# Row maxima of an attention kernel as fp16 parts, split on GpSimd and transposed once

## What is computed

```python
x = x + 0.5 * ffn(layernorm(x))
x = x + attention(layernorm(x))
x = x + 0.5 * ffn(layernorm(x))

# attention: 16 query heads, 4 key/value groups, head size 16, causal
scores = jnp.einsum('bhqd,bhkd->bhqk', q, k) * (1.0 / np.sqrt(d))
scores = jnp.where(causal[None, None, :, :], -jnp.inf, scores)
attn = jax.nn.softmax(scores, axis=-1)
out = jnp.einsum('bhqk,bhkd->bhqd', attn, v)

# feed-forward: weights quantised to three values
hidden = jax.nn.silu(up) * gate
```

## Time and profile before

| | |
|---|---|
| Median of 3 runs | 603.82 us (603.62 to 603.99) |
| Profiled execution | 604.03 us, its span 602.3 us |
| TensorE busy | 566.0 us, 94% of the span |
| VectorE, ScalarE busy | 485.8 us (81%), 412.1 us (68%) |
| GpSimd busy | 176.7 us (29%) |
| Chain that ended last, by engine | PE 79%, DVE 10%, ACT 6% |

### The profile page before, as it was taken

How to read it: one execution, slowest core, us unless ns; L and a number is a source line. 1 busy time by engine, 2 the same in 40 slices (tenths; PEclk the granted TensorE clock), 3 DMA queues, 4 the chain that set the end, 5 groups by cost and what they waited for, 6 DMA issues and landing times.

```text
span 602.3 us, 12457 instructions
## 1 busy us (share of the span) xinstructions
PE 566.0 (94%) x4276; PEld 344.9 (57%) x4276; DVE 485.8 (81%) x1865; ACT 412.1 (68%) x775; POOL 176.7 (29%) x229
## 2 busy tenths in 40 slices
PE   2869999999999989999999999998999999999998
PEld 2336556655666755656566656554445666656666
DVE  6998988889875889888988897888597687756654
ACT  4637756765655378898888888887767656765742
POOL 3015201101530035555545455667501101101100
PEclk9999999999999999999999999999999999999999
DMA  8701001100205151414141424231201111211112
GB/s 313 219 19 35 19 19 36 35 19 19 36 17 125 37 111 56 92 54 93 56 90 58 95 62 92 77 59 30 45 1 36 53 54 36 70 54 53 36 35 71
DMA packets 71679, 37.90 MB, mean 63 GB/s; under 512 B 33984, under 2 KB 71104, under 8 KB 71616
## 3 DMA queue, kind: packets, MB, share of 16 engines
q1 hardware_dynamic: 71616, 37.11, 24.3%
HBM read 18.22 MB, written 10.49 MB: 48 GB/s over the span
## 4 chain that ended last, share of the span: by engine, by line
PE 79%; DVE 10%; ACT 6%; issue 2%; POOL 2%; DMA 1%; DVEq 0%; POOLq 0%; ACTq 0%
PE bank L1112 33%; PE bank L1124 17%; PE bank L1211 7%; PE bank L1279 5%; PE bank L1270 5%; PE bank L1238 5%; ACT shared L566 3%; PE bank L1293 2%; PE bank L1284 2%; DVE sm_out L951 2%; PE bank L1103 1%; DVE hid L814 1%; DVE hl L829 1%; PE bank L1249 1%; POOL xn L395 1%
## 5 line engine op out<-in xcount | busy, mean ns | idle before, releaser
L951 DVE CUSTOM_DVE_ANT_0 sm_out<-bank,mask 128x256 f16<-128x256 f32 (+1 forms) x512 | 153.6, 352 | 25.7 <-PE bank L1238 23.4
L456 ACT ACTIVATE silu<-bank,w_scale 128x512 f32<-128x512 f32 x128 | 87.3, 683 | 117.0 <-PE bank L1112 116.1
L814 DVE SCALAR_TENSOR_TENSOR hid<-silu,h_unit,bank 128x512 f32<-128x512 f32 x128 | 95.0, 742 | 62.5 <-ACT silu L456 62.1
L566 ACT ACTIVATE shared<-bank,qk_scale 128x512 f32<-128x512 f32 x192 | 121.5, 681 | 21.7 <-PE bank L1270 20.8
L1124 PE MATMUL bank<-wT_down,hh 128*128 128x256 f16 x512 | 118.2, 273 | 1.8 <-DVE hl L829 1.6
L1124 PE MATMUL bank<-wT_down,hl 128*128 128x256 f16 x512 | 118.2, 273 | 0.0
L1112 PE MATMUL bank<-xh,wT_gate 128*128 128x512 f16 x256 | 97.1, 379 | 4.4 <-DVE hid L814 4.4
L1112 PE MATMUL bank<-xh,wT_up 128*128 128x512 f16 x256 | 98.0, 383 | 1.2 <-DVE xl L758 1.2
L829 DVE TENSOR_TENSOR hl<-hid,hh 128x512 f16<-128x512 f32 x128 | 98.1, 767 | 0.0
L1112 PE MATMUL bank<-xl,wT_up 128*128 128x512 f16 x256 | 98.0, 383 | 0.0
L404 POOL TENSOR_TENSOR xnl<-xn,xnh 128x1024 f16<-128x1024 f32 x13 | 27.7, 2134 | 238.1 <-ACT xn L493 180.4
(11 more groups left out here) (115 smaller groups left out, 750.3 us busy)
## 6 DMA issues: line engine op xcount, KB each, us to landing
q_st<-q_scratch SPq DMA_DIRECT2D x32, 256.0 KB
q_scratch<-q_hl SPq DMA_DIRECT2D x16, 256.0 KB, 2.2
out_dram<-x SPq DMA_DIRECT2D x7, 512.0 KB, 2.9
x<-in_x_dram SPq DMA_DIRECT2D x1, 3072.0 KB, 15.6
k_scratch<-k_hl SPq DMA_DIRECT2D x16, 128.0 KB, 2.4
k_st<-k_scratch SPq DMA_DIRECT2D x16, 128.0 KB
x<-in_x_dram SPq DMA_DIRECT2D x2, 512.0 KB, 4.6
shared<-in_w_up_t_dram SPq DMA_DIRECT2D x2, 512.0 KB, 6.2
```

What stands on the lines that cost most here:

```text
L456: act.activation(silu[:, e % 2, :], U[e % 2][:, :], ACT.Silu, scale=w_scale[:, 0:1]).then_inc(silu_ready, 1)
L566: act.activation(prob[:, place % 2, i, :], score_bank(n, i)[:, :], ACT.Exp, scale=qk_scale[:, 4:5]).then_inc(exp_done, 1)
L814: dve.scalar_tensor_tensor(out=hid[:, e % 4, :], in0=silu[:, e % 2, :], scalar=h_unit[:, 0:1], in1=GT[e % 2][:, :], op0=ALU.mult, op1=ALU. ...
L951: ins = dve.tensor_tensor_reduce(sm_out[:, i, cols], SM[i][:, cols], mask[:, S - size:S], 1.0, MASKED, ALU.add, ALU.max, rowmax[:, seq_par ...
```

## The change

The split of the maxima moves ahead of the transposes. VectorE now takes the minimum of the negated and scaled scores, so that `rowmax` holds minus the maximum in the units of the product. At the head of groups 0 and 2, ahead of the masks, GpSimd makes both fp16 parts from it in the layout of the queries (`max_parts`: a conversion and a subtraction of 128x16, with a wait of its own between them). TensorE transposes both parts and both query tiles at once (fp16, 128x32) in groups 1 and 3, ScalarE copies the 32x128 result once, ahead of the copy of the outputs (VectorE does so in the one place where it copies the outputs), and SyncE loads rows of 128 instead of 256 elements, in groups 1 and 3. `q_st` has an axis of its own for the sequence, and the scratch read of the second sequence is issued in group 1 of the next even sequence.

```diff
-        q_st = sb("q_st", [P, 2, H, TC], F16)
+        q_st = sb("q_st", [P, 2, 2, H, S], F16)
...
-                sp.wait_ge(mxlo_ready, 2 * b + half + 1)
+                sp.wait_ge(mx_ready, 2 * b + half + 1)
...
-                    sp.dma_start(q_st[64 + part:65 + part, par, heads, cols],
-                                 mx_hl[:, half, part, :]).then_inc(mx_loaded[half], 16)
+                    sp.dma_start(q_st[64 + part:65 + part, par, seq, heads, :].rearrange("o h (t q) -> o (h t) q", t=QT),
+                                 mx_hl[part * QT * HH:(part + 1) * QT * HH, half, :]).then_inc(mx_loaded[half], 16)
...
-                        if g in (0, 2) and not (last and k == 3):
-                            if last and k == 2 and g == 2:
+                        if g in (1, 3) and not (last and k == 3):
+                            if last and k == 2 and g == 3:
                                 x_parts(NC, 0)
                             load_max(b + 1, k + 1, g // 2)
...
-                            sp.wait_ge(st_ready, 3 * G * (b + 1))
-                            read_scratch(c + 2, par, 1)
+                        if not odd and g == 1 and (k or pair) and not (last and k):
+                            sp.wait_ge(st_ready, 3 * G * b)
+                            read_scratch(c + 1, 1 - par, 1)
...
+            step(pool.tensor_copy(ident16[:, :], ident32[:, :]))
...
-            def max_rest(b, half):
-
-                pool.wait_ge(mx_ready, 2 * b + half + 1)
-                if not isinstance(b, int) or b > 0:
-                    pool.wait_ge(mx_loaded[half], 32 * b)
-                pool.tensor_tensor(mx_hl[:, half, 1, :], mx_32[:, half, :], mx_hl[:, half, 0, :],
+            def max_parts(b, half):
+
+                pool.wait_ge(sm_done, 3 * (G * b + 2 * half + 2))
+                if b:
+                    pool.wait_ge(mxT_ready, 2 * b + half - 1)
+                heads = rowmax[:, b % 2, :, half * HH:(half + 1) * HH].rearrange("p t h -> p h t")
+                pool.tensor_copy(mx_q[:, half, 0, :, :], heads).then_inc(mxhi_ready, 1)
+                pool.wait_ge(mxhi_ready, 2 * b + half + 1)
+                pool.tensor_tensor(mx_q[:, half, 1, :, :], heads, mx_q[:, half, 0, :, :],
                                    ALU.subtract).then_inc(mxlo_ready, 1)
...
+                        if g in (0, 2) and not end:
+                            max_parts(b + 1, g // 2)
                         if odd and g in (2, 3):
                             add_output(b - 1, g - 2, 3 - g)
                         if not (end and g == 3):
                             causal(4 * b + g + 1, (g + 1) % 2)
-                        if g in (0, 2) and not end:
-                            max_rest(b + 1, g // 2)
...
-                act.activation(mx_hl[:, half, 0, :], maxima[0:HH, :], ACT.Copy, scale=-1.0 / MAX_UNIT)
-                act.activation(mx_32[:, half, :], maxima[0:HH, :], ACT.Copy,
-                               scale=-1.0 / MAX_UNIT).then_inc(mx_ready, 1)
+                act.activation(mx_hl[:, half, :], maxima, ACT.Copy).then_inc(mx_ready, 1)
...
-                        if g in (0, 2) and not end:
+                        if g in (1, 3) and not copied_by_vector(n):
                             max_copy(b + 1, g // 2)
...
-                    ins = dve.tensor_tensor_reduce(sm_out[:, i, cols], SM[i][:, cols], mask[:, S - size:S], 1.0, MASKED,
-                                                   ALU.add, ALU.max, rowmax[:, seq_par, qt, h:h + 1])
+                    ins = dve.tensor_tensor_reduce(sm_out[:, i, cols], SM[i][:, cols], mask[:, S - size:S], -1.0 / MAX_UNIT,
+                                                   -MASKED, ALU.add, ALU.min, rowmax[:, seq_par, qt, h:h + 1])
...
+                            if k == 2:
+                                dve.wait_ge(mxT_ready, 2 * b + 4)
+                                dve.wait_ge(mx_loaded[1], 32 * b)
+                                dve.tensor_copy(mx_hl[:, 1, :], MT).then_inc(mx_ready, 1)
...
-            def max_transposes(b, k, half):
-                pe.wait_ge(sm_done, 3 * (G * b + 2 * half + 2))
-                if not (isinstance(b, int) and b == 0 and half == 0):
+            def max_transposes(b, half):
+                pe.wait_ge(mxlo_ready, 2 * b + half + 1)
+                if b + half:
                     pe.wait_ge(mx_ready, 2 * b + half)
-                for qt in range(QT):
-                    ins = pe.transpose((FIRST_MT if isinstance(b, int) and b + half == 0 else MT)[0:HH, qt * P:(qt + 1) * P], rowmax[:, k % 2, qt, half * HH:(half + 1) * HH],
-                                       ident32[:, :])
-                ins.then_inc(mxT_ready, 1)
+                pe.transpose(MT if b + half else FIRST_MT, mx_q[:, half, :, :, :].rearrange("p a h t -> p (a h t)"),
+                             ident16[:, :]).then_inc(mxT_ready, 1)
...
-                        if g in (0, 2) and not end:
-                            max_transposes(b + 1, k + 1, g // 2)
+                        if g in (1, 3) and not end:
+                            max_transposes(b + 1, g // 2)
```

38 lines of the change are left out of this document (20 added, 18 removed).

## The result

| | before | changed |
|---|---|---|
| time, median of the runs | 603.9 us (603.62 to 604.39) | 600.09 us (599.85 to 602.01) |
| ratio to before, 95% interval | | 0.9942 (0.9929 to 0.9954) |
| span of the profiled execution | 602.3 us | 598.1 us |
| granted clock | 1.00 | 1.00 |

The change gains 3.8 us where 7.7 were forecast. The time lies inside the range, at its upper end, but half of the forecast gain is missing. The question of the experiments is where it went.

A forecast was written before the change was run, and what follows sets the result against it. TensorE was taken to bound attention, busy 28.01 of 29.51 us in a chunk. Chunks -5.1, start -0.16, last pair -1.6 and its third sequence -0.8 sum to -7.7 us, forecasting 596.2 us, range 594.6 to 600.8.

The forecast's parts named there:

- rival 2: SyncE: the load of the row maxima arrives late and TensorE waits before a half's scores; about 605 to 613 us; chance 0.11.
- Rival 1: Attention: late VectorE row maxima and dearer ScalarE copies keep half the gain away; 599 to 600 us; chance 0.22.
- six chunks: Attention chunks: -0.77 us each with the ScalarE-bound stretch, -0.93 without, three of each kind; -5.1 us.
- last pair, all sequences: Last two-sequence pieces of attention, without projections: -1.6 us from transposes and copies, and -0.8 us with the third sequence.
- Transposes: TensorE: two fp32 transposes of 0.21 us give way to one fp16 of 0.055; 0.155 us per half, 0.62 per chunk.
- ScalarE, group 3 of the odd sequences: With no maxima copies in group 2 of odd sequences, the exponential on the chain starts earlier: -0.28 us per chunk.
- ScalarE, the inserted copies: New maxima copy in odd sequences: +0.16 us in group 1 where ScalarE bounds, +0.16 in group 3; bounds 0.10 and 0.26.
- Even sequences, group 1: A projection no longer waits for an x copy held behind group 0's maxima copies on ScalarE: -0.13 us per chunk.
- Third sequence of the last pair: TensorE's 0.70 us wait for row maxima moves to GpSimd; with gains of the first two groups -0.8 us, bounds 0 and 1.5.
- Start: At the start of attention, the first transposes save 0.16 us.

## Why the prediction was wrong

**The step that failed** is the sentence on SyncE: "The second sequence's scratch read, moved to group 1 of the next even sequence, no longer stands with the first one ahead of the loads; the first one's still does, and the load behind it has about 2 us." The order was seen, and the slack was read well: the comparison of the two traces gives 2.0 us. But the price of standing behind the read was never set against it. It was counted as nothing, and in the four places of the chunks in which TensorE waited it is 2.3 to 4.3 us: the waits of 0.26 to 2.32 us, and the slack. 0.3 to 0.9 us of it is the later issue where the write of the scratch was in time, and 2.0 and 3.0 where the write was late; 1.2 to 1.9 us is the longer landing, which goes with the read's bytes. With 0.75 us in the last pair the waits are 5.2 us; the run with the read behind the load gives 3.8 back in the medians, with a new wait of 0.9.

The mechanism was even on the list, as rival 2: "the load of maxima arrives late", from "a landing 0.3 us (last pair) or 0.5 us (odd sequences) later". I looked for it in the small pieces of the load and in the places with the least slack, and gave it all 30 halves and a slower kernel. It came where a large transfer stands in front, and four of these places have a slack of 2.0 us, more than the last pair and the odd sequences that I watched. The pieces of 256 bytes decided nothing: with the order put right, a transfer of a load lands in the median 1.7 us after its issue (all 64 issues of the trace), and a load in five of the six places 2.3 from the first of its two, as the pieces of 512 bytes did in 2.2. On this the Trainium skill, page "DMA: Bandwidth & Descriptors", was weighed in the prediction, and these runs side with its section "Why small descriptors are slow (HBM only)", by which transfers within SBUF are exempt.

**Rival 1** gives nearly the measured time (599 to 600) for a reason that did not occur: VectorE and ScalarE took back nothing, and the waits of the score matmuls for ScalarE fell from 5.6 us in 13 places to 1.9 in 5.

**The terms**, read from the run with the read behind the load, where no load is late in the chunks:

| term | forecast | measured |
|---|---|---|
| six chunks (first output matmul of group 0 to that of group 3 of the last chunk) | -5.1 | -6.7 |
| last pair, all sequences | -2.4 | -2.3 (0.36 lost at the very end counted in; -1.4 with the new wait) |
| waits for the loads, as changed | 0 | +5.2 |

That the kernel with the read behind the load comes to 596.26 us, where 596.2 was forecast for the changed one, is in part luck: the chunks gave 1.6 us more than their term, and the new wait took 0.9 of it.

- Transposes: two fp32 ones cost 0.21 us each time, as read from the earlier trace rows; in the chunks the intervals to group 2 of every even sequence and to group 0 of every odd one are shorter by just this. The new one was priced at 0.055 and costs 0.012 to 0.02, since the step from scores to outputs takes nearly the same time with or without it. Over 24 halves this is 0.8 to 1.0 of the 1.6 us by which the chunks gained more than forecast. The earlier trace rows gave the step of a matmul in a row of its own kind, and I took it for a change of kind.
- ScalarE, group 3 of the odd sequences: the exponential that was to start 0.28 us earlier does; with the transpose at nearly nothing, the interval went from 2.77 to 2.51.
- ScalarE, the inserted copies: in group 1 of the odd sequences, where ScalarE is the bound, the step is 0.12 to 0.13, with 0.16 forecast. In group 3 of the chunks I put +0.16, and the interval behind it shows 0.03 (4.71 to 4.53, less the 0.21 of transposes). The copy of the outputs had 0.13 us to spare there (a second copy then costs its 0.16 in full). This is 0.8 us over six chunks; with the 0.8 to 1.0 of the transposes it makes up the 1.6. It was read from the last pair, where the groups are shorter.
- Even sequences, group 1: -0.13, as forecast.
- Third sequence of the last pair: the interval to group 2 fell from 3.36 to 2.74, and the chain runs as described, from the row maxima over GpSimd's two instructions and the mask to the outputs. The next interval is 0.22 us longer; the four of that sequence together lose 0.97 us, where 0.8 was forecast. GpSimd's two instructions take 0.20 and 0.22 us, as chosen.
- Start: -0.16 forecast. The first group of attention starts at times that differ by 0.9 us between runs whose work up to there is the same, so this can't be read.

What stays open: how much of each single wait is due to instruction packets. They are seen in the writes ahead of the two largest, and in the late loads near the end of two runs, but no run here took them away. Nor did one part the read's bytes from the number of its packets.

## What to carry to other kernels

When an instruction that issues a transfer moves past another in a queue, write down both orders and price the new one: what the transfers now ahead cost in issue and in bytes, and what they themselves wait for, against the slack of the one behind. A slack alone, without the price beside it, says nothing. And a small, urgent transfer belongs ahead of a large one with time to spare; where the large one has little, its first part may go ahead into a stretch in which the queue is idle.
